# A selective-state step and its read-out on parts of the TensorE array, merged quantiser scales, and a norm moved ahead of a SiLU, in the last phase of a four-layer kernel

## The chip, the cores and the metric

The kernel runs on one core of a Trainium2 chip. The metric is the device time in microseconds (us) of one execution. TensorE, VectorE, ScalarE, GpSimd and the DMA queues of SP run their own instruction streams and wait for each other by semaphores.

## What is computed

Sixteen sequences of 256 tokens with 128 channels pass four residual blocks, each behind a layer norm: gated linear attention, a mixture of eight experts plus a shared expert, a convolution with a small linear state, and a feed-forward block whose activations and weights are quantised to FP4 in blocks of 16. The change touches the third and the fourth, cut here to what matters:

```python
# block 3 (D_INNER 256, D_STATE 16, D_CONV 4)
xp, z = jnp.split(x @ w_in, 2, axis=-1)
xc = silu(causal_conv(xp, conv_w) + conv_b)
def step(h, xt):
    h = h * 0.9 + 0.1 * (xt @ w_B)      # the state, 16 numbers for a sequence
    return (h, h @ w_C)                 # its read-out, 256 channels
_, ys = lax.scan(step, h0, xc.transpose(1, 0, 2))
y = (ys.transpose(1, 0, 2) * silu(z)) @ w_out
# block 4
def fp4_quant_dequant(x):               # blocks of 16 along the last dim
    scale = jnp.maximum(jnp.max(jnp.abs(xb), axis=-1, keepdims=True) / 6.0, 1e-12)
    xn = xb / scale
    q = _GRID[jnp.searchsorted(_MID, jnp.abs(xn))] * jnp.sign(xn) * scale
h = silu(fp4_linear(x, w_gate)) * fp4_linear(x, w_up)
out = fp4_linear(h, w_down)
```

## The kernel before

`phase_ab` does attention, the norm behind it, the routing and part of the experts; `phase_c` the routed experts, and it also fetches and prepares the weights of the last two blocks; `phase_d`, from 367 us on, does blocks 3 and 4. All activations x stay on chip. The order of every engine's instructions is written out by hand, one body for each engine and step j, with semaphores between them.

`phase_d` works on one sequence at a time, skewed over a pipeline. In step j, ScalarE, VectorE and TensorE work on sequence e = j + 4 (first norm), a = j + 3 (convolution, state input, gate), b = j + 2 (state scan's read-out, output projection, second norm, first quantiser), c = j + 1 (gate and up projection, second quantiser) and d = j (down projection, store). j runs from -4 to 15: single steps up to 0, five turns of a hardware loop of two steps each for 1 to 10, then single steps. A piece runs only where its sequence exists. In the first steps the engines also carry what is left of the shared expert (`late_up`, `late_down`, `late_hidden`, `late_add`).

The path of the state in one step. TensorE convolves sequence a into the banks ps_A and ps_Z (twelve matmuls each), ScalarE applies SiLU to each half (`state_silu`, line 1821, into d_xs), TensorE's `gate_half` for each half waits for that half's SiLU, because it writes into the same bank. Between the two gate halves TensorE multiplies both halves of d_xs by wb (line 2170): two accumulating fp32 matmuls with 16 weight columns, into 16 partitions of ps_M. ScalarE copies the result to d_us with the factor 0.1 (line 1878), VectorE scans it to d_hs (line 2017), TensorE multiplies d_hs by wc for the two halves of the channels (line 2098, weights of 128 rows, of which 16 aren't zero) into ps_Y and ps_U, VectorE multiplies by the gate to d_yz (line 1963).

Behind it: the output projection (2120) into ps_M, the addition to x (1980), the second norm (statistics on VectorE, `norm_sums` on GpSimd, lines 1768 to 1775, and the scaled copy xn4 on ScalarE, line 1859, which the profile names d_xn), the first quantiser d_fx on VectorE (maximum 1373, scale 1375, reciprocal 1377, product 1379, rounding 1382 and 1383 around a magnitude on ScalarE, 1361, and the product 1357 to d_xq), the transposes of d_xq (2105), the copy and the low part d_xqT (1832, 1967), the gate and up projection, d_silu (1843), d_hid (1996), the second quantiser d_fh on VectorE for two token tiles, its last product d_hq on GpSimd (1357), the transposes of d_hq (2147), and the down projection (2186).

What an engine has in its queue sets the order around the change. ScalarE's step ends: first half's state SiLU, the norm of b, second half's state SiLU, the two magnitudes of d_fh, the gate's first SiLU, the magnitude of d_fx, d_us, the gate's second SiLU, the norm of e. VectorE has, after d_hid: the four first operations of d_fh for both tiles, four of d_fx, 1382 for both, 1382 for d_fx, the scan, 1383, 1357, the addition to x (2023), and in the next step d_yz, 1967, 1971, statistics and 1383 of d_fh.

fp32 matmuls appear in the profile as two records, one for each pass. The weights wb and wc come by DMA in `phase_c` (`weights`, SP's queue), where GpSimd waits for all of them on one semaphore before it builds the convolution's weights.

## Time and profile before

| | us |
|---|---|
| median of 3 runs | 595.88 |
| lowest, highest run | 594.62, 598.72 |
| the profiled execution: its time | 594.81 |
| its span, first to last instruction | 593.0 |
| the last phase in it | from 367 to the end |

Busy time and its share of the span, from the page of the profile, and the 40 equal slices (a digit is tenths):

```profile
PE 548.3 (92%) x4645; PEld 451.7 (76%) x4646; DVE 443.7 (75%) x1197; ACT 318.8 (54%) x915; POOL 340.6 (57%) x518
PE   7799999999999898976999997988999999999986
DVE  4799889998987359931456742459989998999884
PEclk9999999999999999998899999999999999999999
```

PE is TensorE's matmuls, PEld its weight loads, DVE VectorE, ACT ScalarE, POOL GpSimd. The last phase is the last 15 slices. Matmuls are pipelined: a record's duration reaches from its start to its modelled end, while the next may start earlier, so the time that one takes is read from the distance of the starts. The same holds for VectorE and ScalarE in small measure: the next operation starts a little before the end of the one before, unless it waits for its result.

### The profile page before, as it was taken

The numbers are of one execution on the slowest core, as the hardware profiler recorded it, in microseconds if no ns is written. First come the engines' busy times: TensorE is split into PE (matmuls) and PEld (weight loads), VectorE is DVE, ScalarE is ACT, GpSimd is POOL, SyncE is SP. The second block draws the span as 40 slices with busy tenths as digits, with TensorE's granted clock in tenths as the row PEclk, the third lists the DMA queues.
The fourth block names the chain that finished last, engine by engine and source line by source line (L and its number), as shares of the span: only waits on it lengthen the run. The fifth ranks groups of instructions, "written<-read, shape, count | busy, mean of one in ns | idle before, by whom it ended". The sixth has DMA issues, their size and how long they took to land. (4 is left out here: it accounts for less than half of the span.)

```text
span 593.0 us, 15497 instructions
## 1 busy us (share of the span) xinstructions
PE 548.3 (92%) x4645; PEld 451.7 (76%) x4646; DVE 443.7 (75%) x1197; ACT 318.8 (54%) x915; POOL 340.6 (57%) x518
## 2 busy tenths in 40 slices
PE   7799999999999898976999997988999999999986
PEld 7566677677677577865999896877888888888876
DVE  4799889998987359931456742459989998999884
ACT  3466566666675653313566652444565556555632
POOL 5677777777777422246457401855677676764322
PEclk9999999999999999998899999999999999999999
DMA  7000011001100183001442301211111111110000
GB/s 220 28 30 28 29 38 44 27 27 40 40 27 28 57 225 87 0 28 44 109 110 62 45 27 32 27 15 15 18 20 23 31 18 18 22 31 11 11 18 19
DMA packets 36747, 25.57 MB, mean 43 GB/s; under 512 B 4768, under 2 KB 33632, under 8 KB 36704
## 3 DMA queue, kind: packets, MB, share of 16 engines
q1 hardware_dynamic: 30400, 19.98, 11.5%
q0 software_dynamic: 5888, 4.72, 5.2%
q8 instruction: 21, 0.34, 0.2%
q10 hardware_dynamic: 416, 0.34, 0.2%
q14 instruction: 22, 0.18, 0.1%
HBM read 14.09 MB, written 6.75 MB: 35 GB/s over the span
## 5 line engine op out<-in xcount | busy, mean ns | idle before, releaser
L1180 PE MATMUL a_ps_a<-a_qx,a_kt 32*128 32x512 f32 x512 | 67.3, 613 | 1.6 <-DMA a_qx<-a_qs 1.4
L1753 POOL DMA_INDIRECT x<-yg_dram,pos x32 | 55.1, 1722 | 11.6 <-issue 11.6
L440 POOL TENSOR_SCALAR_AFFINE_SELECT a_at<-a_at 128x512 f32<-128x512 f32 x80 | 51.0, 656 | 13.8 <-ACT a_at L527 13.6
L199 POOL DMA_INDIRECT rows<-xn_dram,slot_token x40 | 40.2, 1005 | 32.2 <-ACT c_rows L1519 18.6
L1357 POOL TENSOR_TENSOR d_hq<-d_fh_v,d_fh_scale 128x352 f32<-128x352 f32 x32 | 27.9, 889 | 51.7 <-DVE d_fh_v L1383 51.7
L1562 DVE TENSOR_TENSOR c_hid<-c_act,c_ps 128x352 f32<-128x352 f32 x39 | 20.2, 519 | 42.8 <-ACT c_act L1505 35.6
L527 ACT ACTIVATE a_at<-a_ps_a 128x512 f32<-128x512 f32 x80 | 44.5, 600 | 10.6 <-PE a_ps_a L1180 9.1
L1180 PEld LDWEIGHTS a_ps_a<-a_qx,a_kt 32*128 32x128 f32 x512 | 31.3, 184 | 16.9 <-issue 16.3
L1505 ACT ACTIVATE c_act<-c_ps 128x352 f32<-128x352 f32 x39 | 17.9, 463 | 38.1 <-PE c_ps L209 29.2
L719 DVE TENSOR_TENSOR a_at<-a_ps_a,mask 128x512 f32<-128x512 f32 x48 | 32.8, 685 | 4.9 <-PE a_ps_a L1180 4.1
L1620 PE MATMUL c_ps_y<-w,c_hidT 128*128 (+1 forms) x234 | 31.8, 287 | 3.4 <-issue 1.8
L1104 PE MATMUL a_ps_o<-a_at,a_vpad 128*32 128x128 f32 x1024 | 34.6, 276 | 0.0
L1620 PEld LDWEIGHTS c_ps_y<-w,c_hidT 128*128 128x128 f32 (+1 forms) x234 | 29.2, 200 | 4.4 <-issue 4.3
L466 POOL TENSOR_TENSOR a_kt<-a_e,a_rope 128x512 f32<-128x512 f32 x16 | 20.4, 1278 | 18.1 <-ACT a_e L563 18.1
L207 PE MATMUL c_ps<-w13p,c_xT 128*128 x74 | 27.9, 376 | 1.6 <-DVE c_hid L1562 0.7
L804 DVE RECIPROCAL a_c<-a_c 128x128 f32<-128x128 f32 x32 | 29.1, 939 | 0.0
L1104 PEld LDWEIGHTS a_ps_o<-a_at,a_vpad 128*32 128x32 f32 x1024 | 26.0, 109 | 3.4 <-issue 3.0
L663 ACT ACTIVATE a_act<-a_ps_a 128x512 f32<-128x512 f32 (+1 forms) x18 | 10.7, 596 | 31.0 <-PE a_ps_a L209 30.9
L1770 POOL TENSOR_TENSOR d_rstd<-d_rstd,halves 128x2 f32<-128x2 f32 x32 | 25.1, 784 | 2.7
L2186 PE MATMUL d_ps_G<-d_wd,d_hqT 128*128 128x128 f32 (+1 forms) x192 | 24.1, 275 | 0.8 <-ACT d_hqT L1851 0.8
L428 POOL TENSOR_TENSOR a_rstd<-a_rstd,halves 128x2 f32<-128x2 f32 x32 | 23.2, 723 | 2.7
L209 PE MATMUL c_ps<-w13p,c_xT 128*128 x74 | 24.5, 332 | 0.0
(357 smaller groups left out, 1831.8 us busy)
## 6 DMA issues: line engine op xcount, KB each, us to landing
a_qx<-a_qs SPq DMA_DIRECT2D x62, 64.0 KB, 1.9
a_at<-in_L_ffn_w_eDF_dram SPq DMA_DIRECT2D x16, 176.0 KB, 2.9
yg_dram<-c_y SPq DMA_DIRECT2D x19, 128.0 KB
xn_dram<-a_xn2s SPq DMA_DIRECT2D x16, 128.0 KB, 1.8
out_dram<-x SPq DMA_DIRECT2D x16, 128.0 KB, 1.9
x<-in_L_attn_x_dram SPq DMA_DIRECT2D x2, 768.0 KB, 6.6
w<-in_L_ffn_w_eFD_dram SPq DMA_DIRECT2D x2, 512.0 KB, 5.3
rows<-xn_dram,slot_token POOLq DMA_INDIRECT x40
```

The source lines that it names most:

```text
L199: nc.gpsimd.indirect_dma_start(out=g["rows"][:, k % 4, t, :], out_offset=None, in_=g["xn2_dram"][:, :], in_offset=bass.IndirectOffsetOnAxi ...
L207: nc.tensor.matmul(to, left(0), right(0), start=start, stop=False)
L440: nc.gpsimd.affine_select(at[:, t, r, :, :], at[:, t, r, :, :], pattern=[[0, 4], [1, P]], compare_op=ALU.is_ge, fill=0.0, base=0, channel_ ...
L527: nc.scalar.activation(at[:, t, r, :, :], ps_a[:, r, :, :], ACT.Copy).then_inc(s_copied, 1)
L719: nc.vector.tensor_tensor(at[:, t, r, :, :], ps_a[:, r, :, :], mask[:, 0:1, :].to_broadcast([P, 4, P]), ALU.mult).then_inc(s_masked, 1)
L804: nc.vector.reciprocal(c[:, tile(t)], c[:, tile(t)]).then_inc(s_rc, 1)
L1104: last = nc.tensor.matmul(ps_o[32 * r:32 * r + 32, tile(t)], vpad[:, b.par, t, c0:c0 + 32], at[:, t, r, h, :], start=(t == 0 and h == 0), ...
L1180: last = nc.tensor.matmul(ps_a[:, r, :, :], kt[rows, b.par, c_, tile(t)], qx[rows, b.par, :, c_, tile(t)], start=(c_ == 0), stop=(c_ == 1))
L1357: return eng.tensor_tensor(self.by(to), self.by(self.v[:, :]), self.spread(self.scale), ALU.mult)
L1620: last = nc.tensor.matmul(ps_y[:, t, :], hidT[0:fn, f.par, t, n, :], w2[0:fn, e_out[t], n, :], start=(n == 0), stop=(n == 2))
L1753: nc.gpsimd.indirect_dma_start(out=x[:, t, :], out_offset=None, in_=g["yg_dram"][:, :], in_offset=bass.IndirectOffsetOnAxis(ap=g["pos"][:, ...
L1770: nc.gpsimd.tensor_tensor(to, to, halves[:, 0:2], ALU.pow).then_inc(s_n, 1)
```

## The change

In five edits, all but the fetch of two weights in the last phase:

1. State input on column tiles. wb is padded with zeros to 32 columns. Each half of d_xs is multiplied twice, into two groups of 32 partitions of ps_M (half 0 into partitions 0 and 64, half 1 into 32 and 96): four fp32 matmuls that accumulate nothing, instead of two that do. ScalarE's copy d_us and VectorE's scan d_hs then work on 128 partitions; the two halves are added later.
2. Read-out on row tiles. wc lies four times in its tile, at partitions 0, 32, 64 and 96. The matmul of channel half h takes the 64 rows from 64h on, in d_hs and in wc, and sums both halves of the state input.
3. The second quantiser's maxima, scales and reciprocals of the two token tiles lie side by side; scale and reciprocal are one operation for both tiles each, after both maxima.
4. On ScalarE the norm of b stands in front of the first half's state SiLU instead of behind it.
5. wc is fetched by four transfers instead of one, a memset for wb comes in, the memset of d_hs goes, since the scan writes all of it.

```diff
-                "wb": sbm("wb", [P, 2, DS]),
+                "wb": sbm("wb", [P, 2, 32]),
...
-                    sp.dma_start(g["wc"][0:DS, :], io["L1_attn_w_C"]).then_inc(s_w, 16)
+                    for q in range(4):
+                        sp.dma_start(g["wc"][32 * q:32 * q + DS, :], io["L1_attn_w_C"]).then_inc(s_w, 16)
...
+            nc.gpsimd.memset(g["wb"][:, :, :], 0.0).then_inc(s_zero, 1)
             for k in range(3, 14):
                 rows_for(k)
-            pool.wait_ge(s_w, 16 * 7)
+            pool.wait_ge(s_w, 16 * 10)
...
-        decay = sb("decay", [DS, N])
+        decay = sb("decay", [P, N])
...
-        us = sb("us", [DS, N])
+        us = sb("us", [P, N])
...
-        fp4_h = [Fp4(nc, sb, f"fh{t}", F) for t in range(2)]
+        both = [sb(f"fh_{n}", [P, 2, F // QB]) for n in ("amax", "scale", "inv")]
+        fp4_h = [Fp4(nc, sb, f"fh{t}", F, [a[:, t, :] for a in both]) for t in range(2)]
...
-            nc.gpsimd.memset(hs[:, :], 0.0).then_inc(s_wz, 1)
...
-                if live(a):
-                    wait(act, s_u, a, ago=1)
-                    state_silu(a, 0)
                 if live(b):
                     wait(act, s_nb4, b, n=4, per=4)
...
                 if live(a):
+                    wait(act, s_u, a, ago=1)
+                    state_silu(a, 0)
+                if live(a):
                     state_silu(a, 1)
...
-                    nc.scalar.activation(us[:, :], ps_M[0:DS, 0:N], ACT.Copy, scale=0.1).then_inc(s_us, 1)
+                    nc.scalar.activation(us[:, :], ps_M[:, 0:N], ACT.Copy, scale=0.1).then_inc(s_us, 1)
...
+            amax, scale, inv = (a[:, :, :].rearrange("p t b -> p (t b)") for a in both)
...
+            def hidden_scales(c):
+
+                wait(dve, s_hq, c, n=2, per=2, ago=1)
+                dve.wait_ge(s_qz, c.lin(PER, 2))
+                nc.vector.tensor_scalar(scale, amax, -1.0 / 6.0, -1e-12, ALU.mult, ALU.min).then_inc(s_qz, 1)
+                dve.wait_ge(s_qz, c.lin(PER, 3))
+                nc.vector.reciprocal(inv, scale).then_inc(s_qz, 1)
...
-                    for n in range(4):
-                        for t in range(2):
-                            hidden_step(c, n, t)
+                    for t in range(2):
+                        hidden_step(c, 0, t)
+                    hidden_scales(c)
+                    for t in range(2):
+                        hidden_step(c, 3, t)
...
-                    nc.vector.tensor_tensor_scan(hs[0:DS, :], decay[:, :], us[:, :], 0.0, ALU.mult, ALU.add).then_inc(s_scan, 1)
+                    nc.vector.tensor_tensor_scan(hs[:, :], decay[:, :], us[:, :], 0.0, ALU.mult, ALU.add).then_inc(s_scan, 1)
...
-                        nc.tensor.matmul((ps_Y, ps_U)[h][:, 0:N], wc[:, P * h:P * h + P], hs[:, :], start=True, stop=True).then_inc(s_yp, 1)
+                        rows = slice(64 * h, 64 * h + 64)
+                        nc.tensor.matmul((ps_Y, ps_U)[h][:, 0:N], wc[rows, P * h:P * h + P], hs[rows, :], start=True, stop=True).then_inc(s_yp, 1)
...
-                        last = nc.tensor.matmul(ps_M[0:DS, 0:N], wb[:, h, :], xs[:, h, :], start=(h == 0), stop=(h == 1))
+                        for c0 in (32 * h, 32 * h + 64):
+                            last = nc.tensor.matmul(ps_M[c0:c0 + 32, 0:N], wb[:, h, :], xs[:, h, :], start=True, stop=True)
                     last.then_inc(s_u, 1)
```

ScalarE's order in a full step of the last phase, from the last hidden transpose's copy on. Before (a row is the line, the operation, output and inputs, partitions x elements):

```order
L1851 ACTIVATE d_hqT<-d_ps_Y 96x128
L1821 ACTIVATE d_xs<-d_ps_A,cb 128x256
L1859 ACTIVATE d_xn<-x,d_shift,d_rstd 128x128 x2
L1821 ACTIVATE d_xs<-d_ps_Z,cb 128x256
L1361 ACTIVATE d_fh_k<-d_fh_v 128x352 x2
L1825 ACTIVATE d_zs<-d_ps_A 128x256
```

and after the change, at the same place (the lines have moved by one or two):

```order
L1853 ACTIVATE d_hqT<-d_ps_Y 96x128
L1858 ACTIVATE d_xn<-x,d_shift,d_rstd 128x128 x2
L1823 ACTIVATE d_xs<-d_ps_A,cb 128x256
L1823 ACTIVATE d_xs<-d_ps_Z,cb 128x256
L1361 ACTIVATE d_fh_k<-d_fh_v 128x352 x2
L1827 ACTIVATE d_zs<-d_ps_A 128x256
```

The norm of b (d_xn) now runs before the first of the two SiLUs (d_xs from d_ps_A), and both SiLUs stand next to each other.

VectorE's order at the second quantiser, before:

```order
L1996 TENSOR_TENSOR d_hid<-d_silu,d_ps_Z 128x352
L1373 TENSOR_REDUCE d_fh_amax<-d_hid 128x22 x2
L1375 TENSOR_SCALAR d_fh_scale<-d_fh_amax 128x22 x2
L1377 RECIPROCAL d_fh_inv<-d_fh_scale 128x22 x2
L1379 SCALAR_TENSOR_TENSOR d_fh_v<-d_hid,d_fh_inv 128x352 x2
L1373 TENSOR_REDUCE d_fx_amax<-d_xn 128x16
```

and after:

```order
L2007 TENSOR_TENSOR d_hid<-d_silu,d_ps_Z 128x352
L1373 TENSOR_REDUCE d_fh_amax<-d_hid 128x22 x2
L1948 TENSOR_SCALAR d_fh_scale<-d_fh_amax 128x44
L1950 RECIPROCAL d_fh_inv<-d_fh_scale 128x44
L1379 SCALAR_TENSOR_TENSOR d_fh_v<-d_hid,d_fh_inv 128x352 x2
L1373 TENSOR_REDUCE d_fx_amax<-d_xn 128x16
```

Nothing else moves there; four small operations have become two, each of which reads what the one before it writes.

## Rows read from the trace of the kernel before

**Rows 1.** Busy time by engine, 458 to 482 us (record counts behind x).

```profile
458.00:482.00 24.00, 23.57 (x162) 19.96 (x162) 22.24 (x74) 14.04 (x40) 16.66 (x25) 1.00 0.13 22
```

**Rows 2.** TensorE timeline: start, duration (us), line, operation, tiles, shapes.

```profile
478.62 0.28 PE L209 MATMUL d_ps_A<-d_xnT,wmix 128*128 128x256 f32 x1
...
478.83 1.04 PE L2170 MATMUL d_ps_M<-d_xs,wb 128*16 128x256 f32 x4
...
479.79 0.39 PE L207 MATMUL d_ps_Z<-d_xnT,wmix 128*128 128x256 f32 x1
...
480.25 1.50 PE L2186 MATMUL d_ps_G<-d_wd,d_hqT 128*128 128x128 f32 x12
...
481.66 0.70 PE L2098 MATMUL d_ps_Y<-d_hs,wc 128*128 128x256 f32 x2
...
482.62 0.38 PE L2105 MATMUL d_ps_T<-mask,d_xq 128*128 128x128 f32 x2
```

**Rows 3.** The same view in the first phase, matmuls on 128x32 tiles.

```profile
168.22 1.08 PE L1104 MATMUL a_ps_o<-a_at,a_vpad 128*32 128x128 f32 x32
...
169.23 0.71 PE L1119 MATMUL a_ps_m<-a_vpad,a_ktok 128*128 128x128 f32 x4
```

**Rows 4.** TensorE weight loads, timeline; the bracket is idle time and its releaser.

```profile
479.10 0.26 PEld L2170 LDWEIGHTS d_ps_M<-d_xs,wb 128*16 128x16 f32 x2 [0.17 <-ACT d_xs L1821]
```

**Rows 5.** ScalarE timeline, same iteration.

```profile
477.15 0.47 ACT L1821 ACTIVATE d_xs<-d_ps_A,cb 128x256 f32<-128x256 f32 x1 [0.89 <-PE d_ps_A L209]
...
478.58 0.47 ACT L1821 ACTIVATE d_xs<-d_ps_Z,cb 128x256 f32<-128x256 f32 x1 [0.19 <-PE d_ps_Z L209]
...
479.99 0.42 ACT L1361 ACTIVATE d_fx_k<-d_fx_v 128x256 f32<-128x256 f32 x1
```

**Rows 6.** GpSimd timeline, same iteration.

```profile
476.84 0.22 POOL L1775 TENSOR_SCALAR d_shift<-d_shift 128x2 f32<-128x2 f32 x1 [0.16 <-POOL d_shift L1772]
```

**Rows 7.** VectorE timeline, same iteration and the start of the next.

```profile
475.54 0.94 DVE L1373 TENSOR_REDUCE d_fh_amax<-d_hid 128x22 f32<-128x352 f32 x2
...
476.39 0.32 DVE L1375 TENSOR_SCALAR d_fh_scale<-d_fh_amax 128x22 f32<-128x22 f32 x2
...
476.97 0.93 DVE L1379 SCALAR_TENSOR_TENSOR d_fh_v<-d_hid,d_fh_inv 128x352 f32<-128x352 f32 x2
...
478.43 0.42 DVE L1373 TENSOR_REDUCE d_fx_amax<-d_xn 128x16 f32<-128x256 f32 x1 [0.53 <-ACT d_xn L1859]
...
478.88 0.18 DVE L1375 TENSOR_SCALAR d_fx_scale<-d_fx_amax 128x16 f32<-128x16 f32 x1
...
479.38 0.42 DVE L1379 SCALAR_TENSOR_TENSOR d_fx_v<-d_xn,d_fx_inv 128x256 f32<-128x256 f32 x1
...
480.59 0.42 DVE L1382 SCALAR_TENSOR_TENSOR d_fx_sum<-d_fx_k,d_fx_v 128x256 f32<-128x256 f32 x1
...
480.93 0.67 DVE L2017 TENSOR_TENSOR_SCAN d_hs<-d_decay,d_us 16x256 f32<-16x256 f32 x1
...
481.95 0.42 DVE L1357 TENSOR_TENSOR d_xq<-d_fx_v,d_fx_scale 128x256 f32<-128x256 f32 x1
...
483.46 0.42 DVE L1967 TENSOR_TENSOR d_xqT<-d_ps_T,d_xqT 128x256 fp32r<-128x256 f32 x1
```

**Rows 8.** Instructions of line 782, the first phase's scans: minimum, median, maximum ns.

```profile
L782 DVE TENSOR_TENSOR_SCAN a_c<-ones,a_de,a_e x16: 1187/1296/1351, 13.0 to 184.1; 128x128 f32<-128x128 f32 x16
...
L782 DVE TENSOR_TENSOR_SCAN a_c<-ones,a_init,a_e x16: 483/484/485, 14.4 to 185.7; 128x128 f32<-128x128 f32 x16
```

**Rows 9.** GpSimd timeline in the third phase.

```profile
307.94 0.40 POOL L1486 COPY c_wtap<-c_win 128x256 f32<-128x256 f32 x1 [1.47 <-DMA wc<-in_L_attn_w_C_dram]
```

**Rows 10.** ScalarE timeline in the ramp of the last phase.

```profile
394.12 0.88 ACT L1859 ACTIVATE d_xn<-x,d_shift,d_rstd 128x128 f32<-128x128 f32 x2 [1.20 <-POOL d_shift L1775]
```

**Rows 11.** TensorE timeline in the same ramp.

```profile
393.61 0.28 PE L207 MATMUL d_ps_A<-d_xnT,wmix 128*128 128x256 f32 x1
...
399.44 0.41 PE L2105 MATMUL d_ps_T<-mask,d_xq 128*128 128x128 f32 x2 [0.25 <-DVE x L1904]
```

More of the change, by code:

```diff
@@ L1338, with __init__ @@
 class Fp4:
-    def __init__(self, nc, sb, name, width):
+    def __init__(self, nc, sb, name, width, small=None):
         self.nc, self.width, self.blocks = nc, width, width // QB
-        self.amax, self.scale, self.inv = (sb(f"{name}_{n}", [P, self.blocks]) for n in ("amax", "scale", "inv"))
+        self.amax, self.scale, self.inv = small or [sb(f"{name}_{n}", [P, self.blocks]) for n in ("amax", "scale", "inv")]
         self.v, self.k, self.sum = (sb(f"{name}_{n}", [P, width]) for n in ("v", "k", "sum"))
@@ L1935, in hidden_step @@
                 else:
[L1936 to L1938 removed]
+                    dve.wait_ge(s_qz, c.lin(PER, 7 + t))
                 fp4_h[t].step(n, hid[:, t, :]).then_inc(s_qz if n < 5 else s_qh, 1)
+            def hidden_scales(c):
[4 more added lines that the diff above has]
+                nc.vector.reciprocal(inv, scale).then_inc(s_qz, 1)
             def input_step(b, n):
```

19 lines of the change are left out of this document (9 added, 10 removed).

## The prediction

> **What bounds the kernel now.** The change touches only the last phase (from 367 us to the end), so I read first how busy each engine is there and then one iteration engine by engine. In two iterations of 12 us TensorE is busy 23.57 of 24 us and VectorE 22.24 [rows 1]: both are near full, and neither has to be the bound by itself. The timeline shows what closes the circle. Call T the two transposes of line 2105. From T the way goes to ScalarE (d_xqT), VectorE (line 1967 and, queued behind it, line 1383), GpSimd (d_hq) and back to TensorE, whose second set of hidden transposes waits for d_hq. This half holds no work of the change. From those transposes to the next T (7.5 us) TensorE works almost without a gap: convolution, gate, state input (L2170), gate, down projection, read-out (L2098). What is saved in that half moves the period one for one, until another input of T or of line 1967 is the late one. So I price each edit by T, at 482.62 us in the iteration shown [rows 2].
>
> **State input, twice as many matmuls on column tiles.** Before, four passes (two per fp32 matmul) start at 478.83 and the gate's matmul follows at 479.79 [rows 2]: 0.96 us, of which a pass takes 0.215 and about 0.10 is emptying the array. The same 0.10 stands before it: 478.62 to 478.83 instead of the usual 0.12. So the before, with its 16-column weights, already pays both switches, and only the passes count. In the first phase 32 passes of 128 columns on 128x32 tiles take 168.22 to 169.23, 1.01 us, where a pass of that length alone takes half of 0.215: they run four abreast [rows 3]. After the change the first half's pair runs abreast in two passes, and the second pair uses other column tiles, but it cannot start before ScalarE has its d_xs, at 479.10 [rows 4]. It then takes 0.43 + 0.10, to 479.65 instead of 479.79: **-0.14**. If nothing ran abreast it would be 8 passes, +0.86.
>
> **Read-out on row tiles.** Today it is 0.96 us from 481.66 to T, four passes and a weight load of 0.10 that shows because the load waits for the scan, which ends at 481.60 [rows 2, 7]. On 64-row tiles the two matmuls run abreast, 0.43 us. But now the array changes shape before and after, 0.10 each, and the first weight load shows, 0.10. By itself that is 0.73 to 0.83 against 0.86 to 0.96. Trainium skill, TensorEngine Tiling (Array Packing), Theoretical Speedup: a small dimension up to 64 gives up to 2x; by that the read-out would give 0.43 instead of about 0.13. The same page, Key Properties, says that a change of tiling mode drains the engine, and the trace's 0.10 agrees. No row here has 64-row tiles; the bounds are no overlap (+0.3) and 0.43 saved.
>
> **Norm in front of the state's SiLU.** ScalarE runs the first SiLU at 477.15 and only then the norm; GpSimd's shift is ready at 477.06 [rows 5, 6]. After, the norm (a pair, 0.88 [rows 10]) goes at 477.11, is done at 477.99, and VectorE's line 1373 starts at 478.03 instead of 478.43, where it now ends a wait of 0.53 [rows 7]. The first SiLU ends near 478.37 instead of 477.6. Queued behind it is TensorE's first gate product, which starts at 478.38 (two products of 0.12 ahead of the one at 478.62 [rows 2]): its weight load comes late, about 0.14. That costs nothing, since the second half of the state input waits for the second SiLU at 479.10 anyway, and that one (478.58, released by TensorE) finds ScalarE free with 0.3 to spare. But ScalarE is then full from 478.58 to its d_fx_k at 479.99 + 0.42 [rows 5], so VectorE's line 1382 can start at 480.45, not 480.19: of the 0.40 won, **0.14** is left for the scan, d_xq and all behind them.
>
> **Merged scales.** Two pairs of small operations become two operations of 44 columns. The pairs take 0.58 us together (476.39 to 476.97) and hide their latency in each other: the first scale starts at 476.39, while the second maximum runs to 476.48 [rows 7]. The merged ones are serial. The other quantiser shows what that costs: 0.45 from maximum to scale, then 0.50 for scale and reciprocal [rows 7]. Merged, the scale starts 0.03 after the second maximum, at 476.51; with 28 more columns scale and reciprocal take about 0.24 + 0.32, and line 1379 starts at 477.07 instead of 476.97: **+0.10**, not a saving. Trainium skill, VectorE: DVE Perf Modes, Rules for kernel authors: minimise the operation count, not the semaphores; by that rule two operations fewer would save about 0.3. Either is hidden: line 1379's pair then ends at 478.00, just ahead of the 478.03 at which the norm arrives. Without that cover it would cost the 0.10 whole.
>
> **Scan and copy on 128 partitions.** The copy d_us has the same columns, as has the scan (0.67 us at 16 partitions). The nearest scans on 128 partitions take 0.48 and 1.28 us for 128 columns, one instruction at two prices [rows 8]. I take 0.67, as two of the first kind can't need more than 0.97, and keep 1.28 as the bad end.
>
> **Weights.** Three more small transfers on SP delay GpSimd's weight taps, which wait 1.47 us for wc's transfer already, at 307.94 [rows 9]; that wait about doubles. Behind the wait stand row gathers, issued four pairs ahead, and wmix, read only in the last phase: nothing. One memset goes, one comes, both away from the path.
>
> **The sum for one iteration.** The scan ended at 481.60 [rows 7], now 481.46. TensorE's down projection (twelve passes of 0.11 from 480.25 [rows 2]) ended near 481.59, now 481.45; 0.10 to empty the array gives 481.55, then 0.10 + 0.43 + 0.10: 482.18. T also needs d_xq, 482.37 before, 482.23 now [rows 7]; with 0.04 for the semaphore and 0.06 of a late load T starts at 482.33 instead of 482.62. Line 1967 behind it: it follows T by 0.84 today (483.46 [rows 7]), so 483.17, and VectorE, 0.14 earlier and without its last 0.16 of waiting, is free at 483.16. So **-0.29**, and both chains are used up: more on TensorE would not bring more. That circle closes 13 times, for the transposes T after the first two.
>
> **The ramp.** One iteration loses. The norm at 394.12 comes after 1.20 us of waiting for GpSimd, and the first SiLU ran before that wait [rows 10]. After, the SiLU stands behind the norm: it starts at 394.9 and is done at 395.4. TensorE's gate product, at 393.61 [rows 11], moves to 395.5, and behind it stand two halves of the late down projection, the state input, the read-out and T at 399.44. Of the 1.9 us, 0.43 come back in the state input (both halves ready), and 0.25 from T's wait [rows 11]: **+1.2**. The iterations before and after it should gain 0.3 each, by the same parts as the sum above (one has no norm, the other waits for the scan).
>
> Sum: 13 x -0.29 = -3.8, +1.2, -0.6: **-3.2 us**. The profiled execution took 594.81 us (span 593.0), so 591.6 on its terms; it stands 1.07 below the median of 595.88, from which I forecast **592.7**.
>
> **Rivals.**
> B, the gain is taken by ScalarE. The second SiLU has only 0.3 to spare; should the norm pair come 0.5 later in each iteration than I place it, the SiLU, d_fx_k and T would slip with it and about 0.1 remain: -1.3 + 1.2 - 0.3 = -0.4, 595.5 us. For it: the ramp shows the mechanism at full size. Against: in the steady rows GpSimd is ready at 477.06.
> C, the whole of VectorE's wait comes back. If the merge does save and the ScalarE chain has give, 0.50 per iteration: -6.5 + 0.6, 590.0. For it: VectorE's 0.53 [rows 7]; against: d_fx_k at 479.99 stands between.
> D, slower: the tiles don't run abreast, since the pairs are two deep and not four as in rows 3. The state input then ends at 480.8 instead of 479.79, +1.0, and the read-out is +0.3 for its switches: 13 x 1.3, about 613. It decides once 0.8 of that 1.3 is real (+0.5 net per iteration, with the ramp over 1%).
> E, slower: the scan costs 1.28, +0.6 in VectorE's chain: 13 x (0.6 - 0.2) + 0.6 = +5.8, 601.7. Against: the dear scans are only those of one half of rows 8.
> That the edits do nothing is B.
>
> **How the numbers follow.** A (my sum) 0.62, with its own range 590.5 to 594.8; B 0.20; C 0.10; D 0.04; E 0.04. A measurement of this kernel can tell about 1%, 6 us, from no change. Faster by that (below 589.9): half of C and the low tail of A, 0.08. Slower (above 601.8): D and half of E, 0.06. The range takes A and B, and reaches down to C's value and up to B's with the run-to-run spread: 589.9 to 596.6.
>
> **What would show it.** State input: the four passes' place shrinks to about 0.8 us with eight records; read-out: 0.4 us of records with 0.1 us gaps on both sides. Merge: 1.1 us from the second maximum to line 1379's place. VectorE's wait before its d_fx_amax gone, a new one before d_fx_sum (ScalarE). The period of two iterations falls by about 0.6, and the first T of the ramp comes about 0.9 later. A fall of 0.2 or less makes B right, one of 1.0, C; a scan row above 1 us, E.

## The result: half a per cent slower in one comparison, though each iteration is as much shorter as predicted

| | before | changed |
|---|---|---|
| median | 595.79 us | 598.51 us |
| lowest, highest run | 594.62, 598.72 | 594.37, 601.62 |
| the profiled execution | 594.81 | 594.37 |
| its span, mean granted clock | 593.0, 0.991 | 592.6, 0.997 |

Ratio 1.0045 of the medians; 1.004 with the 95% interval 1.0025 to 1.0055. The change is inside the 1% below which the prediction takes a difference as none, and outside its range (589.9 to 596.6). Two things disagree from the start: the traced execution of the changed kernel is 0.44 us faster than that of before, the median is 2.7 us slower.

Busy time in the same 24 us as [rows 1], and then in 96 us (eight iterations) of both kernels, in the order PE, PEld, DVE, ACT, POOL, granted clock, DMA share, GB/s. The changed kernel's two rows:

```profile
458.00:482.00 24.00, 23.28 (x177) 19.50 (x176) 23.40 (x71) 14.71 (x44) 16.53 (x25) 1.00 0.13 22
458.00:554.00 96.00, 92.91 (x694) 77.38 (x693) 93.53 (x281) 57.90 (x167) 59.05 (x94) 1.00 0.12 21
```

And of the kernel before, with the one group of VectorE's waits of that stretch that is over 1 us; the changed kernel has no group at all there:

```profile
458.00:554.00 96.00, 94.32 (x644) 79.92 (x644) 89.12 (x291) 56.15 (x160) 60.63 (x93) 1.00 0.12 21
DVE d_fx_amax L1373 <- ACT d_xn L1859: 4.5, 8, 0.6
```

Before, VectorE waited 0.56 us per iteration for the norm; now it is busy 93.53 of 96 us and the view shows no wait of it. TensorE fell from 94.32 to 92.91 although more iterations lie in the window. The bound has passed from TensorE to the chain of VectorE and ScalarE, as the rows below show.

The steady iteration, TensorE of the changed kernel (it answers to [rows 2]):

```profile
479.43 0.39 PE L207 MATMUL d_ps_A<-d_xnT,wmix 128*128 128x256 f32 x1
...
479.77 0.28 PE L209 MATMUL d_ps_A<-d_xnT,wmix 128*128 128x256 f32 x1
479.98 0.71 PE L2185 MATMUL d_ps_M<-d_xs,wb 128*32 128x256 f32 x8
480.62 0.39 PE L207 MATMUL d_ps_Z<-d_xnT,wmix 128*128 128x256 f32 x1
...
481.08 1.50 PE L2201 MATMUL d_ps_G<-d_wd,d_hqT 128*128 128x128 f32 x12
482.51 0.48 PE L2112 MATMUL d_ps_Y<-d_hs,wc 64*128 64x256 f32 x1
482.52 0.48 PE L2112 MATMUL d_ps_U<-d_hs,wc 64*128 64x256 f32 x1
482.83 0.38 PE L2112 MATMUL d_ps_Y<-d_hs,wc 64*128 64x256 f32 x1
482.84 0.38 PE L2112 MATMUL d_ps_U<-d_hs,wc 64*128 64x256 f32 x1
483.30 0.44 PE L2119 MATMUL d_ps_T<-mask,d_xq 128*128 128x128 f32 x2
```

The weight load of T in it:

```profile
483.30 0.20 PEld L2119 LDWEIGHTS d_ps_T<-mask,d_xq 128*128 128x128 f32 x2 [0.48 <-DVE d_xq L1357]
```

Eight passes now fill 0.64 us (479.98 to 480.62), where four filled 0.96. In the read-out the pairs start 0.01 us apart: both products run abreast. Read-out to T is 0.79 instead of 0.96, and T now waits for VectorE's d_xq, so 0.79 is not the read-out's own length. That shows in the ramp, where the next product of the whole array (L2127, before L2113) waits for nothing. The changed kernel, then the kernel before (before_again, the same wait in front of it):

```profile
389.62 0.45 PE L2112 MATMUL d_ps_Y<-d_hs,wc 64*128 64x256 f32 x1 [1.49 <-DVE d_late_hid L1900]
...
390.26 0.44 PE L2127 MATMUL d_ps_H<-mask,d_xn 128*128 128x128 f32 x2
```

```profile
381.48 0.67 PE L2098 MATMUL d_ps_Y<-d_hs,wc 128*128 128x256 f32 x2 [1.49 <-DVE d_late_hid L1898]
...
382.42 0.38 PE L2113 MATMUL d_ps_H<-mask,d_xn 128*128 128x128 f32 x2
```

There the read-out takes 0.64 us with its switches, on the whole array 0.94.

VectorE in the same iteration (to be read beside [rows 7]):

```profile
476.49 0.94 DVE L1373 TENSOR_REDUCE d_fh_amax<-d_hid 128x22 f32<-128x352 f32 x2
477.46 0.20 DVE L1948 TENSOR_SCALAR d_fh_scale<-d_fh_amax 128x44 f32<-128x44 f32 x1
477.70 0.43 DVE L1950 RECIPROCAL d_fh_inv<-d_fh_scale 128x44 f32<-128x44 f32 x1
478.16 0.96 DVE L1379 SCALAR_TENSOR_TENSOR d_fh_v<-d_hid,d_fh_inv 128x352 f32<-128x352 f32 x2
479.05 0.42 DVE L1373 TENSOR_REDUCE d_fx_amax<-d_xn 128x16 f32<-128x256 f32 x1
...
480.43 0.96 DVE L1382 SCALAR_TENSOR_TENSOR d_fh_sum<-d_fh_k,d_fh_v 128x352 f32<-128x352 f32 x2
481.39 0.43 DVE L1382 SCALAR_TENSOR_TENSOR d_fx_sum<-d_fx_k,d_fx_v 128x256 f32<-128x256 f32 x1
481.74 0.68 DVE L2030 TENSOR_TENSOR_SCAN d_hs<-d_decay,d_us 128x256 f32<-128x256 f32 x1
482.34 0.45 DVE L1383 SCALAR_TENSOR_TENSOR d_fx_v<-d_fx_k,d_fx_sum 128x256 f32<-128x256 f32 x1
482.82 0.42 DVE L1357 TENSOR_TENSOR d_xq<-d_fx_v,d_fx_scale 128x256 f32<-128x256 f32 x1
```

No row has a bracket, but one wait is hidden in them. d_fx_sum starts 0.96 behind the start of the pair ahead of it (480.43 to 481.39); before it was 0.87, from this row to the 480.59 of [rows 7]:

```profile
479.72 0.95 DVE L1382 SCALAR_TENSOR_TENSOR d_fh_sum<-d_fh_k,d_fh_v 128x352 f32<-128x352 f32 x2
```

It starts 0.03 behind the end of ScalarE's d_fx_k (480.95 + 0.41, below), and does so in eight of the nine iterations from the fourth T to the thirteenth, where before 0.19 or 0.25 lay between them. So VectorE waits 0.09 us for ScalarE here. From the first maximum to line 1379 it takes 1.67 us, before 1.43 [rows 7]: the merge costs 0.24. The scan on 128 partitions takes 0.68, before 0.67.

ScalarE and GpSimd of the changed kernel there ([rows 5, 6]):

```profile
478.14 0.88 ACT L1858 ACTIVATE d_xn<-x,d_shift,d_rstd 128x128 f32 x2 [0.93 <-POOL d_shift L1777]
478.93 0.45 ACT L1823 ACTIVATE d_xs<-d_ps_A,cb 128x256 f32<-128x256 f32 x1
479.54 0.47 ACT L1823 ACTIVATE d_xs<-d_ps_Z,cb 128x256 f32<-128x256 f32 x1 [0.16 <-PE d_ps_Z L209]
...
480.95 0.41 ACT L1361 ACTIVATE d_fx_k<-d_fx_v 128x256 f32<-128x256 f32 x1
```

```profile
477.79 0.22 POOL L1777 TENSOR_SCALAR d_shift<-d_shift 128x2 f32<-128x2 f32 x1 [0.16 <-POOL d_shift L1774]
```

**Where the time went.** I followed the sixteen T of both traces. Changed minus before, in us: +2.49 at the first (401.93 against 399.44), +1.84 at the fourth, -0.75 at the thirteenth, -1.09 at the fifteenth, -0.69 at the last, -0.44 at the end. From the fourth to the thirteenth the mean period is 11.655 us, before 11.943: **-0.29**. (Long and short iterations alternate; away from the ends a pair takes 23.32, before 23.87, which is -0.27 each.) So the loss lies ahead of the first T: +0.44 in the first two phases, which the change doesn't touch, +1.3 in the third phase, +0.74 in the ramp. The ramp's rows, ScalarE and then TensorE (they answer to [rows 10, 11]):

```profile
395.35 0.88 ACT L1858 ACTIVATE d_xn<-x,d_shift,d_rstd 128x128 f32<-128x128 f32 x2 [4.23 <-POOL d_shift L1777]
396.13 0.45 ACT L1823 ACTIVATE d_xs<-d_ps_A,cb 128x256 f32<-128x256 f32 x1
```

```profile
396.64 0.38 PE L207 MATMUL d_ps_A<-d_xnT,wmix 128*128 128x256 f32 x1 [1.66 <-ACT d_xs L1823]
...
401.93 0.41 PE L2119 MATMUL d_ps_T<-mask,d_xq 128*128 128x128 f32 x2 [0.24 <-DVE x L1906]
```

The SiLU stands behind the norm, the norm waits 4.23 us for GpSimd, and TensorE idles 1.66 us for the SiLU, about as predicted. The third phase has what I had put at nothing, GpSimd's wait ([rows 9]: 1.47), and two waits of TensorE's weight loads behind it:

```profile
310.39 0.40 POOL L1488 COPY c_wtap<-c_win 128x256 f32<-128x256 f32 x1 [3.52 <-DMA wc<-in_L_attn_w_C_dram]
```

```profile
321.99 1.42 PEld L1622 LDWEIGHTS c_ps_y<-w,c_hidT 128*128 128x128 f32 x12 [0.68 <-issue]
...
328.12 1.41 PEld L1622 LDWEIGHTS c_ps_y<-w,c_hidT 128*128 128x128 f32 x12 [1.63 <-issue]
```

The kernel before has one such wait there:

```profile
329.52 0.30 PEld L1645 LDWEIGHTS c_ps_h<-mask,c_hid 128*128 128x128 f32 x3 [1.36 <-DVE c_hid L1562]
```

**And the median?** The mean granted clock of each of the 20 executions of the changed kernel is on record: 0.974 to 0.997, median 0.983. Their times fall on a line against it (correlation -0.91): 0.94 us for each 0.003 of clock, 598.3 us at 0.983, 595.8 at 0.991. The traced one, at 0.997, is the fastest of the twenty. Of before only the traced execution's clock is known in this comparison, 0.991, with a time 1.0 below its median; in the later comparisons the clock of every execution of both is on record.

### The profile page after: what moved, and what is told of

Same layout as the page of the kernel before. It is cut to its first block and busy times, and to the rows that moved or that the text cites. A ratio compares the mean times of both kernels' runs of the same rounds, so it can differ in the third digit from the quotient of the medians.

```text
span 592.6 us, 15556 instructions
## 1 busy us (share of the span) xinstructions
PE 539.8 (91%) x4709; PEld 441.7 (75%) x4710; DVE 448.4 (76%) x1165; ACT 318.3 (54%) x915; POOL 336.2 (57%) x518
## 5 line engine op out<-in xcount | busy, mean ns | idle before, releaser
L1756 POOL DMA_INDIRECT x<-yg_dram,pos x32 | 53.2, 1662 | 12.0 <-issue 12.0
L207 PE MATMUL c_ps<-w13p,c_xT 128*128 x74 | 27.5, 372 | 1.7 <-DVE c_hid L1564 0.7
L207 PE MATMUL d_ps_A<-d_xnT,wmix 128*128 128x256 f32 x80 | 25.1, 313 | 2.6 <-ACT d_xs L1823 1.9
```

The source lines that it names most:

```text
L207: nc.tensor.matmul(to, left(0), right(0), start=start, stop=False)
L1756: nc.gpsimd.indirect_dma_start(out=x[:, t, :], out_offset=None, in_=g["yg_dram"][:, :], in_offset=bass.IndirectOffsetOnAxis(ap=g["pos"][:, ...
```

## The experiments

All compared with the kernel before on the same chip. Two kinds of chip turned up: on chips 0, 2, 6 and 7 the kernel before takes 587.8 to 588.4 us, on chip 9 595.4. The chip of the first comparison is not on record; its 595.8 puts it with chip 9. The difference is in the third phase: its first twelve row pairs take 50.0 us there, 57.5 here.

**Is the result the same elsewhere? after_again, after_third, after_fourth: the changed kernel unedited; before_again: the kernel before.**

> The changed kernel once more, for more executions with the clock of each. Theory K (clock): its time follows the mean granted clock, about 1 us for each 0.003, and it loses to the kernel before because it is granted less; then its executions at 0.99 and above take 594 to 596 us, those at 0.98 take 599 to 600, and its median is 597.5 to 599. Theory P (path): the loss is work and waits that every execution has; then executions at equal clock are slower than those of the kernel before by the full 2 to 3 us.

> The kernel before, unchanged, in the same rounds, for its clocks. Theory K: its mean granted clock lies at 0.988 to 0.992 in nearly all executions, above that of the changed kernel. Theory P: both have the same clocks.

> The changed kernel once more, beside the kernel before and its variants. The saving in the steady iterations must be there in every execution (period of two iterations 23.3 us against 23.86). Theory that the first comparison (ratio 1.0045) was the ramp plus stretches at 1.2 GHz that come in some executions: the ratio lies anywhere from 0.997 to 1.005, and this trace shows a half-clock stretch between 380 and 406 us or gives a ratio under 1. Rival, a fixed loss outside the last phase: then the third phase is over 1 us longer than before in this trace too.

> The changed kernel once more, as the partner of the three others. Third-phase theory: where GpSimd's copy c_wtap starts behind 308 us it waits over 3 us for wc's transfer and the phase is 1.3 us longer than before; where the same copy comes near 302 us, the phase isn't longer. Ratio 1.002 to 1.005 in the first case, 0.997 to 1.001 in the second.

Measured: 0.9988 (0.9967 to 1.0009) on chip 7, 0.9988 (0.9967 to 1.001) on chip 2, 1.0019 (0.9995 to 1.0044) on chip 9. The period was 11.653 to 11.657 us in every trace of the changed kernel, 11.936 and 11.943 in those of before. So the steady saving is there everywhere; it is the rest that differs.

The clocks test theory K against theory P. For each kernel: executions, their median granted clock, and the mean time of those at 0.991:

| chip | before | changed |
|---|---|---|
| 7 | 33, 0.997, 589.6 us | 12, 0.991, 587.5 us |
| 2 | 29, 0.994, 589.3 us | 12, 0.991, 586.5 us |
| 9 | 35, 0.991, 595.4 us | 12, 0.9895, 596.0 us |

On the quicker kind K holds: at equal clock the changed kernel is 2.1 and 2.8 us faster, and its lower clock takes back 1.1 to 1.4 us of it. (That before would lie at 0.988 to 0.992 was wrong: 8 of its 12 executions in before_again had 0.997.) On chip 9 it is 0.6 slower at equal clock, from two executions of it. after_fourth came out as forecast. after_third didn't: its ratio is over 1 with no stretch at half clock between 380 and 406 us, and its third phase is 1.3 us longer, which is what its rival said.

**The ramp. norm_behind_in_ramp: the old order of norm and SiLU in the first iterations only.**

```
+            def early(j):
+                return j.m is None and j.off <= -2
...
+                if live(a) and early(j):
+                    wait(act, s_u, a, ago=1)
+                    state_silu(a, 0)
                 if live(b):
...
-                if live(a):
+                if live(a) and not early(j):
                     wait(act, s_u, a, ago=1)
                     state_silu(a, 0)
```

> The changed kernel, with ScalarE's norm behind the state's SiLU again in the single steps up to -2, in front of it from then on. The prediction's step on the ramp: the first transpose of line 2119 comes 1.0 to 1.2 us earlier against the start of the phase, and the whole is 1 us faster. Rival: the ramp is bound by something else, less than 0.4 us.

Measured: 584.36 us, **0.9938** (0.9918 to 0.9958), 3.0 us better than the changed kernel in the same comparison. From the third phase's last row pair to the first T it took 45.94 us, against 47.18. That trace of the changed kernel has a stretch at 1.2 GHz at 381 us; in the two that have none between the row pair and T (after, after_fourth) it is 46.96 and 46.97; norm_behind_in_ramp has one too, at 360 us. So by these traces the old order is worth 1.0 to 1.2 us in the ramp, near what was priced. The median granted clock is 0.994, the changed kernel's 0.991, and on the lines through both kernels' executions 2.0 us are left at equal clock: about 1.0 of the 3.0 is clock, and some 0.8 has no place in the traces.

**The wait for wc. taps_own_wait: GpSimd waits only for the two transfers it reads, win and cw** (run three times, on chips 7, 2 and 6).

```
-                    sp.dma_start(win[:, :], io["L1_attn_w_in"]).then_inc(s_w, 16)
+                    sp.dma_start(win[:, :], io["L1_attn_w_in"]).then_inc(s_tap, 16)
...
-            pool.wait_ge(s_w, 16 * 10)
+            pool.wait_ge(s_tap, 32)
```

> The changed kernel, but GpSimd waits, before it builds the convolution's weights, for the two transfers that it reads, not for all ten. Theory W (the three added transfers hold GpSimd, its row gathers come late, TensorE stands still once in the third phase): GpSimd's wait of 3.5 us at 310.4 goes, TensorE's idle of 0.7 and 1.6 us near 322 and 328 goes, and the start of the last phase comes 1.3 to 2 us earlier; 1.3 to 2 us faster than the changed kernel. Rival, as the prediction had it (hidden): no change within 0.5 us.

> GpSimd's taps wait for their own two transfers alone (win, cw); all else is the changed kernel. Third-phase theory: the wait in front of the copy c_wtap and the two late row pairs behind it are gone, and where the changed kernel pays 1.3 us for them, this one is 1.3 us faster than after_fourth. Rival, lost clock is all of the difference: the same median within 0.5 us.

> Where the kernel before takes 595 us: by the third-phase theory the copy c_wtap has no wait, the row pairs behind it come in time, the transposes of the rows at the phase's end are 1.3 us earlier than in the changed kernel's traces there (336.8 and 341.3 us for the two pairs around the losses), and the ratio is 0.9980 to 1.0015 instead of 1.0019 to 1.0045. Rival, the late row pairs come from something else: the phase is 1.3 us longer here too. Where the kernel before takes 588 us it says nothing new: 0.998 to 1.000.

Measured: 0.9983 (0.9968 to 0.9999), 0.9996 (0.9979 to 1.0013), 0.9984 (0.9971 to 0.9998). Forecast was 1.3 to 2 us less than the changed kernel in the first, 1.3 in the second; measured were 0.5 less and 1.7 more, so both missed. The wait is gone, first row; the second is the changed kernel on the same chip:

```profile
298.83 0.42 POOL L1488 COPY c_wtap<-c_win 128x256 f32<-128x256 f32 x1
```

```profile
302.37 0.40 POOL L1488 COPY c_wtap<-c_win 128x256 f32<-128x256 f32 x1 [3.18 <-DMA wc<-in_L_attn_w_C_dram]
```

But it brought nothing. On these chips the two row pairs behind the wait take 9.0 us with the long wait in five traces of six, 9.8 without any and 9.8 in before. In one of the five (norm_behind_in_ramp, with a wait of 3.9) an earlier pair is 0.7 late instead, and in the sixth, tiles_off, the two take 10.0; that kernel fetches wc by one transfer and still waits 2.9 us, since the transfer took 3.6 us to land instead of the 2.2 in before_again. So the length of the wait doesn't hang on the three added transfers alone, and what it does to the row pairs is not explained. On the slower kind four traces with the long wait show 10.6 to 11.0 where before has 10.2, and no variant without the wait ran there. before_taps, the same edit on the kernel before, was meant to say whether it helps by itself:

> The kernel before, with GpSimd's taps waiting for their own two transfers alone. It waits 1.47 us for wc's transfer and its row pairs are not late behind that, so by the third-phase theory this gives nothing: 1.000 +- 0.002, apart from the 1.1 to 1.4 us for which TensorE waits for c_hid once in the phase, which another order of GpSimd's work may move (0.998). Rival, that wait costs the kernel before as well: 0.997 or less, and then the repair would be no part of what the change cost.

0.9988 (0.9974 to 1.0001): nothing that can be told from no change, as forecast.

**Each part alone. norm_behind (no swap anywhere), tiles_off (whole array for both products), readout_whole (column tiles kept, read-out on the whole array), scales_apart (two pairs of scales again).** The cores of the edits, in this order:

```
+                if live(a):
+                    wait(act, s_u, a, ago=1)
+                    state_silu(a, 0)
```

```
-                        for c0 in (32 * h, 32 * h + 64):
-                            last = nc.tensor.matmul(ps_M[c0:c0 + 32, 0:N], wb[:, h, :], xs[:, h, :], start=True, stop=True)
+                        last = nc.tensor.matmul(ps_M[0:DS, 0:N], wb[:, h, 0:DS], xs[:, h, :], start=(h == 0), stop=(h == 1))
```

```
-                        nc.tensor.matmul((ps_Y, ps_U)[h][:, 0:N], wc[rows, P * h:P * h + P], hs[rows, :], start=True, stop=True).then_inc(s_yp, 1)
+                        nc.tensor.matmul((ps_Y, ps_U)[h][:, 0:N], wc[:, P * h:P * h + P], hs[:, :], start=True, stop=True).then_inc(s_yp, 1)
```

```
-                    for t in range(2):
-                        hidden_step(c, 0, t)
-                    hidden_scales(c)
-                    for t in range(2):
-                        hidden_step(c, 3, t)
+                    for n in range(4):
+                        for t in range(2):
+                            hidden_step(c, n, t)
```

> The changed kernel with the norm behind the state's first SiLU again, in every iteration; tiles and merged scales stay. Where the changed kernel stands at 0.9988 of the kernel before. By the walk of the prediction VectorE's d_fx_amax then waits for the norm again (0.4 to 0.5 us) and T is 0.17 later in each steady iteration: the period of two iterations goes from 23.3 back to about 23.65, 13 x 0.17 = +2.2 us, and the ramp gives 1.2 back: about +1.0 us against the changed kernel by the trace, if the granted clock is the same. Theory that the ramp's idle stretch also costs granted clock (the variant with the old order in the ramp alone went to 0.9938, 1.8 us more than its 1.2): then the median is 0.8 below the changed kernel's, a ratio near 0.9975. Rival, the tiles alone give the whole saving of the steady iteration: the period stays at 23.3 and the ratio is that of the variant with the old order in the ramp alone, 0.994.

> The changed kernel with state input and read-out on the whole array and one wc transfer again; norm in front and merged scales stay. By the walk of the prediction 0.14 of the 0.29 are left to T's two chains only if both are shorter: with d_xq 0.14 earlier but the read-out at 0.96, T is 0.14 earlier than before and the period of two iterations 23.6, 13 x 0.13 = 1.7 us slower than the changed kernel: ratio about 1.0015, at equal clock. Rival, the tiles do it all: the period goes to the 23.86 of the kernel before, +3.5 us, ratio 1.005. Rival, the swap does it all: 23.3 and 0.9988.

> The changed kernel with the read-out on the whole array again (two wc copies of four, the scan still on 128 partitions); state input on column tiles, norm in front and merged scales stay. By the walk of the prediction T has two inputs that are equally late, so giving back the read-out's 0.13 or more puts T back: scan 0.14 earlier, read-out 0.96 with no switches, T 0.14 to 0.2 earlier than before instead of 0.29: period of two iterations 23.5 to 23.6, 13 x 0.12 = 1.6 us slower than the changed kernel in the same call. Rival, the read-out's tiles are worth nothing since d_xq is the late one: 23.3. Rival, they are the whole gain: 23.86, +3.5 us.

> The changed kernel with the scales and reciprocals of the second quantiser as two pairs again. By the prediction the merge costs 0.10 us that is hidden: from the second maximum to line 1379's place 0.1 us less, VectorE's busy time in a 24 us window up by about 0.4 us, period of two iterations 23.3 as now, ratio as the changed kernel's, 0.9988 +- 0.002. Rival, VectorE's operations are what the period hangs on (it is busy over 23 of 24 us): the two operations more cost 0.15 to 0.3 us in each of 16 iterations, +2.4 to +4.8 us, ratio 1.003 to 1.007.

| | mean period, us | ratio to before |
|---|---|---|
| before | 11.94 | 1 |
| tiles_off (swap and merge) | 11.97 | 1.0051 (1.0033 to 1.007), chip 0 |
| norm_behind (tiles and merge) | 11.85 | 1.0005 (0.9987 to 1.0023), chip 0 |
| readout_whole | 11.78 | 1.0032 (1.0011 to 1.0053), chip 9 |
| scales_apart (tiles and swap) | 11.68 | 0.9972 (0.995 to 0.9993), chip 0 |
| all four parts | 11.655 | 0.9988 twice, 1.0019 |

Windows of 96 us, in this order: tiles_off, norm_behind, readout_whole; behind the second its wait for the norm:

```profile
458.00:554.00 96.00, 94.05 (x645) 79.90 (x644) 91.64 (x275) 57.21 (x161) 58.67 (x94) 1.00 0.11 19
```

```profile
458.00:554.00 96.00, 92.25 (x688) 77.53 (x686) 90.83 (x272) 57.15 (x164) 56.98 (x92) 1.00 0.11 20
DVE d_fx_amax L1373 <- ACT d_xn L1861: 2.2, 8, 0.3
```

```profile
458.00:554.00 96.00, 94.29 (x692) 80.53 (x692) 93.02 (x277) 58.38 (x167) 59.72 (x95) 1.00 0.12 21
```

Without the tiles VectorE's wait for the norm is gone (no such group in tiles_off), but TensorE is busy 94.05 of 96 as before and the period stays. This missed its forecast, a pair of iterations of 23.6 us; it took 23.9. (norm_behind with 23.65 and readout_whole with 23.56 came out as forecast.) The swap by itself costs TensorE time: the first gate product waits for the later SiLU, the state input starts 8.27 or 8.37 us behind T (the two kinds of iteration) instead of 7.98 or 8.16, and the down projection is 0.2 to 0.3 us late. The column tiles, 0.32 us shorter, pay that back. Without the swap TensorE is relieved, but VectorE waits 2.2 us again. **Neither gives the saving alone: +0.03 and -0.09; together -0.29.** The read-out's tiles are worth 0.13, about what I had expected. The merge is worth 0.02 per steady iteration, but at both ends it costs more: from the first T to the fourth 34.62 us with it and 34.51 in scales_apart, from the thirteenth to the last 34.06 and 33.73, from there to the end 17.12 and 16.83. From the first T to the end the changed kernel takes 190.7 us and scales_apart 190.2, so by these traces the merge loses 0.5 us. Of the rivals, that the tiles do it all falls by norm_behind (in tiles_off it had forecast the right number), that the swap does falls by tiles_off, and that VectorE's number of operations does by scales_apart. What tiles_off lost beyond it is the ramp: 47.86 us to the first T instead of 46.2.

**The granted clock. gap_filled, norm_ramp_filled.** A stretch at 1.2 GHz starts at 381 to 386 us, in the ramp, just behind TensorE's wait of 1.49 us for d_late_hid, in 5 of the 11 traces of kernels that keep the swap in the ramp, in 2 of the 6 with tiles and the old order there, and in none of the 3 of the kernel before or its variant. Two of the 11 have another at 405 to 410. This count isn't all: 15 of the 20 traces, with all three of the kernel before and its variant, have a stretch at 359 to 371 us, at the start of the last phase, and the four of the 11 from the slower kind have none at 381 to 386.

The clocks of all executions say more than one trace of each. In all ten later runs with the swap in the ramp the mean granted clock is 0.0011 to 0.0036 below that of before in the same comparison; in the six with the old order there it lies between 0.0020 below and 0.0011 above. The ranges overlap, but the swap in the ramp goes with a lower clock. The windows of one kernel (norm_ramp_taps, below) on two chips, 6 and 2, with the stretch and without:

```profile
378.00:390.00 12.00, 10.23 (x64) 8.84 (x62) 5.04 (x17) 4.49 (x11) 4.97 (x10) 0.86 0.10 13
```

```profile
378.00:390.00 12.00, 10.23 (x82) 8.52 (x80) 6.02 (x20) 5.22 (x15) 5.88 (x10) 1.00 0.10 13
```

The same busy time holds 64 matmuls or 82, and the first T came 0.87 us later with the stretch. One at 405 us costs 1.29 (three periods of 35.90 instead of 34.61, taps_own_wait). The fillers:

```
                     if b.m is None and b.off == 0:
+                        keep_busy(10)
                         pe.wait_ge(s_lh, 6)
```

> The changed kernel with ten small matmuls (about 1.1 us) on TensorE in the 1.49 us in which it waits for d_late_hid ahead of the ramp's first read-out; nothing else depends on them. In four of the six traces of changed kernels a stretch at 1.2 GHz starts 0.1 to 2 us behind that idle time, in none of the two of the kernel before. Theory of the granted clock: the stretch at 381 to 384 us is gone in the trace, and the median is 1 to 2 us below the changed kernel's in the same comparison. Rival, the stretch has another cause (or the fillers themselves delay the read-out): stretch still there, or median the same within 0.5 us.

> The same ten matmuls, and the old order of norm and SiLU in the ramp. That order alone stood at 0.9938 and 0.9951 of the kernel before, with no half-clock stretch in the ramp in its traces. If the idle time ahead of the read-out costs clock in the executions not traced, this gains 0.5 to 1 us more, ratio 0.992 to 0.993; if the order alone already avoids it, the ratio stays at 0.994 to 0.995.

Measured on chip 9: 1.0034 (1.0011 to 1.0057) and 0.9996 (0.9975 to 1.0017). Both missed their forecasts; the fillers in gap_filled:

```profile
387.03 2.39 PE L2092 MATMUL d_ps_M<-ones 128*128 128x128 f32 x20
```

Ten matmuls are twenty passes and 2.39 us, not 1.1, longer than the 1.49 us gap they were to fill. The first T came 47.67 us behind the third phase, where the changed kernel without a stretch needs 46.96. No stretch showed there, but no other trace from that kind of chip had one at 381 either. So this test doesn't decide what draws the clock down.

**Both repairs. norm_ramp_taps, three times.**

> The old order of norm and SiLU in the iterations of the ramp, and GpSimd's taps waiting for their own two transfers alone. If the two losses are separate: GpSimd's copy c_wtap has no wait, the ramp is 1.2 us shorter than the changed kernel's, and the ratio to the kernel before is 0.993 to 0.994 (the wait for wc's transfer is worth 0 to 0.5 us here). If the wait for wc was what made the third phase longer by 1.3 us in the changed kernel's first trace: 0.991 to 0.992.

> Both repairs together: norm behind the SiLU in the ramp's iterations, taps waiting for their own two transfers. If ramp (1.2) and third phase (1.3) are the two losses and the steady saving (13 x 0.27 = 3.5) is the gain on every chip, this is 2.5 us or more faster than after_fourth where the third phase pays, and about 3 us faster than before: ratio 0.994 to 0.996. If the loss on the slower chips is of another kind: 0.999 or more.

> Both repairs. Where the kernel before takes 595 us the one in the ramp stood at 0.9996 with the third phase 1.3 us longer; without that loss 0.9975. If the wait is not the cause: 0.9996. Where the kernel before takes 588 us: 0.995.

Measured: 0.9951 (0.9932 to 0.997), 0.9946 (0.9927 to 0.9965), 0.9947 (0.9929 to 0.9966), on chips 0, 2, 6; the first is just above its forecast of 0.993 to 0.994, the others are at theirs. No better than norm_behind_in_ramp's 0.9938 on chip 7, so nothing shows that the repair of the taps adds anything. **The version to keep is the change with the old order of norm and SiLU in the ramp**: 3.8 us faster than before on chip 7, and with the taps' repair 2.6 to 3.5 us on three more of the quicker kind. On the slower kind it ran only with the fillers, and was as fast as before. With the scales apart as well it should gain some 0.5 us more by the traces; that kernel did not run.

## Why the prediction was right and wrong

That the difference would stay below 1% was right, the forecast (592.7) and the range were not. By its steps:

- **The period** (-0.29): measured -0.29, but with luck in the match. In the iteration that was walked it fell by 0.22 (11.73 us from T to T; predicted 11.66, before 11.95), in the other kind by 0.31. Counted from the T before, d_fx_amax starts after 7.48 us (predicted 7.36, before 7.76), d_fx_sum after 9.82 (9.78, before 9.92), and d_xq ends after 11.67 (11.56, before 11.70). The order of the waits was right: norm, d_fx_k, d_xq, T, and each came up to 0.12 later than placed. The other kind of iteration, which was not walked, made up for that, and the two at the ends of the nine more so (-0.40 and -0.33).
- **Norm in front, "That costs nothing"**: wrong for TensorE. The first gate product waits for the moved SiLU (end at 478.93 + 0.45) and starts at 479.43, the state input 8.41 us behind T instead of 8.16.
- **State input** (-0.14): the passes ran abreast and its place shrank by 0.32, since the second half's SiLU was ready when it was wanted, but it started 0.25 later. The down projection came 0.07 earlier, not 0.14.
- **Read-out** (0.73 to 0.83): mis-sized. The 0.79 to T is set by d_xq; its own length, from the ramp, is 0.64 against 0.94. From that I estimate that TensorE has about 0.15 us to spare before T (482.51 + 0.64 = 483.15, T at 483.30), so "both chains are used up" holds for VectorE and ScalarE alone.
- **Scan** (0.67): 0.68. D and E fall, as do B and C: two periods fell by 0.55.
- **Merge** (+0.10, hidden): +0.24, and hidden, but only just: line 1379's pair ends at 479.12, the norm at 479.02. I had taken the 44-column scale and reciprocal at 0.24 + 0.32; the reciprocal starts at 477.70 and its reader 0.46 later. Where no norm is late, it is paid: scales_apart wins back 0.33 us in the last three iterations and 0.29 behind them. The last T loses 0.40, and in that iteration VectorE of the kernel before and of the changed kernel read:

```profile
570.25 0.94 DVE L1373 TENSOR_REDUCE d_fh_amax<-d_hid 128x22 f32<-128x352 f32 x2
...
571.73 0.93 DVE L1379 SCALAR_TENSOR_TENSOR d_fh_v<-d_hid,d_fh_inv 128x352 f32<-128x352 f32 x2
```

```profile
569.28 0.94 DVE L1373 TENSOR_REDUCE d_fh_amax<-d_hid 128x22 f32<-128x352 f32 x2
...
571.01 0.96 DVE L1379 SCALAR_TENSOR_TENSOR d_fh_v<-d_hid,d_fh_inv 128x352 f32<-128x352 f32 x2
```

  1.48 us became 1.73. The Trainium skill's rule to minimise the operation count (VectorE: DVE Perf Modes, Rules for kernel authors) would have had it 0.3 shorter; two operations that depend on each other show their whole latency, four in two chains hide it, and here the measurement goes against the rule.
- **"a new one [wait] before d_fx_sum"**: right, and small: 0.09 us, too short for a bracket. d_fx_sum starts 0.03 behind the end of d_fx_k.
- **The ramp** (+1.2): near. norm_behind_in_ramp gives 1.0 to 1.24 back.
- **"The iterations before and after it should gain 0.3 each"** was too much: with the old order in the ramp the first T comes only 0.1 to 0.3 earlier than in before. With the last T's 0.40 and the 0.29 behind it, the sum for the last phase is 1.0 us too good: from the third phase's last row pair to the end it took 2.2 us less than before, where -3.2 was predicted.
- **Weights ("nothing")**: a failed step on the slower kind of chip. The wait did "about double", to 3.2 to 3.5 us, but "issued four pairs ahead" was no cover: the row pairs issued behind it came late, and the phase became 1.3 us longer in the first comparison, and 1.3, 0.6 and 1.4 in after_third, gap_filled and norm_ramp_filled (3.1 in readout_whole, with a stretch at 1.2 GHz in it). On the quicker kind the phase became 0.8 us shorter. That the wait for wc causes the loss was not tested on the chips that show it (taps_own_wait was meant to, and ran on the quicker kind each time), and one trace of before stands against four of changed kernels; it stays the likeliest cause, not a shown one.
- **"it stands 1.07 below the median of 595.88, from which I forecast 592.7"** is the step that put the time out of the range. It takes the distance between a traced execution and the median as a property of the kernel. For the changed kernel it is 4.1 us, since its traced execution had 0.997 and its median execution 0.983; with 1.07 the trace's 594.37 would have given 595.4, inside the range. Of the 5.8 us between 592.7 and 598.5 this step has 3.1. The other 2.8 are the trace against the predicted 591.6: 1.3 in the third phase, 1.0 in the last, 0.44 in the first two.

**How much of the 2.7 us is clock.** At 0.991 the changed kernel's line gives 595.8. Against it stand 594.8, the one traced execution of before, and 595.4, the 16 executions of before at 0.991 on chip 9. So 0.4 to 1.0 us are there at equal clock, and 1.7 to 2.3 are a lower clock. The 0.4 to 1.0 have no place in the traces: the third phase and the last one together are 0.9 us shorter in the changed kernel's. The swap in the ramp, with 1.66 us more of an idle TensorE, costs by itself (norm_behind_in_ramp, 1.0 to 1.2 us) and goes with a lower granted clock in the later comparisons. That the idle time is what lowers the clock is not shown: the experiment that was to isolate it did not, and what draws the clock down stays open.

## What to carry to other kernels

When two chains end together, price an edit by walking both: here tiles alone gave 0.09, an earlier norm alone nothing, and both 0.29 us per iteration, since the earlier norm delays the other chain by what the tiles save. Look at the first and last iterations apart from the steady one: an order that is right in the steady state cost 1.0 to 1.2 us in the ramp, and one condition on the order won 3.0 us back in the median; a merge that is free in the steady state cost 0.5 us at the ends. A sum made against one traced execution says nothing on the clock that the other executions are granted, so a range for the median needs room for it, upwards above all when an edit lets TensorE idle longer.

## What the runs showed of the hardware

- Two 64-row products on different row tiles start 0.01 us apart and their four passes fill 0.33 us of starts; with the switches the place is 0.64 us in the ramp, where the whole array takes 0.94. Eight passes on 32-column tiles fill 0.64 where four on 16 columns filled 0.96.
- A scan of 256 columns takes 0.68 us on 128 partitions and 0.67 on 16.
- The time of one kernel on one chip varies by 7 us with the mean granted clock, 0.94 us per 0.003. A single stretch at 1.2 GHz cost 0.87 us in the ramp and 1.29 us where both TensorE and VectorE are nearly full.
- The same kernel takes 588 us on four chips and 595 on another, nearly all of it in the gathers' phase, and a DMA wait there that is 2 us longer was seen with a phase 0.8 us shorter in four traces of six on the one kind and with one 0.6 to 1.4 us longer on the other.
